# Attention block with routed experts: three issue orders changed (attention rows ahead of an expert's second weights, first half ahead of the differences in the search, two orders in the first selection)

## The reference, cut to what matters

```python
# x [2, 2048, 256]; 16 heads of 16; 8 experts of 128 slots, hidden 1024
h = _layernorm(x) * (1 + ca) + sa
q, k, v = heads(h @ Wq + bq), heads(h @ Wk + bk), heads(h @ Wv + bv)
scores = einsum('bhqd,bhkd->bhqk', q, k) * scale
sparsity = scores.max(-1) - scores.mean(-1)
_, top_idx = top_k(sparsity, 307)                 # per batch and head
attn = softmax(q[top_idx] @ k.T * scale)
out = zeros_like(q).at[top_idx].set(attn @ v)
x = x + ga * (merge(out) @ Wo + bo)

h = _layernorm(x) * (1 + cb) + sb
xn, sn = rmsnorm(h), rmsnorm(slot_embeds)
logits = einsum('bnd,esd->bnes', xn, sn)
dispatch, combine = softmax(logits, over n), softmax(logits, over e*s)
slots = einsum('bnd,bnes->besd', xn, dispatch)
eo = gelu(slots @ w1[e] + b1[e]) @ w2[e] + b2[e]
x = x + gb * einsum('bmd,bnm->bnd', eo, combine)
```

## Time and profile before

| | |
|---|---|
| runs, median | 1568.8 us (1565.49 to 1570.86) |
| profiled execution | 1565.02 us |
| its span | 1563.3 us |
| PE busy | 1456.9 us (93%) |
| DVE busy | 1214.3 us (78%) |
| ACT busy | 1042.3 us (67%) |
| POOL busy | 242.9 us (16%) |
| chain that ended last | PE 49%, DVE 34%, issue 11%, DMA 3%, ACT 2%, POOL 1% |

### The profile page before, as it was taken

The page is one execution under the profiler, slowest core; times in us unless marked ns, Lnnn a source line. Parts: engine busy times, 40 slices in busy tenths (PEclk is TensorE's granted clock), DMA queues, the critical chain, the costliest instruction groups (busy, mean ns, idle before and its releaser), DMA issues.

```text
span 1563.3 us, 28260 instructions
## 1 busy us (share of the span) xinstructions
PE 1456.9 (93%) x8706; PEld 802.8 (51%) x8706; DVE 1214.3 (78%) x2841; ACT 1042.3 (67%) x1452; POOL 242.9 (16%) x289
## 2 busy tenths in 40 slices
PE   7999999998989989999999889999999999999999
PEld 3542222223444432222222644444889986489988
DVE  5679999999897769999999888977855534775411
ACT  4578888887767778888888448864433463443453
POOL 1540000000720051111111212232111000011100
PEclk9999999999999999999999899999999999999999
DMA  5861111112432201111112212201243202024410
GB/s 178 267 170 41 41 40 41 41 43 84 148 119 79 69 18 50 48 42 42 42 42 82 71 40 60 54 24 46 94 162 126 95 30 74 1 85 153 136 49 32
DMA packets 93811, 119.40 MB, mean 76 GB/s; under 512 B 23054, under 2 KB 79118, under 8 KB 93212
## 3 DMA queue, kind: packets, MB, share of 16 engines
q1 hardware_dynamic: 91164, 117.66, 24.8%
q0 software_dynamic: 2560, 0.66, 0.2%
HBM read 93.46 MB, written 24.82 MB: 76 GB/s over the span
## 4 chain that ended last, share of the span: by engine, by line
PE 49%; DVE 34%; issue 11%; DMA 3%; ACT 2%; POOL 1%; SPq 0%; DVEq 0%; ACTq 0%
DVE work_area L1326 26%; PE psum L2181 7%; PE psum L2122 7%; PE psum L2245 7%; PE psum L2040 5%; PE psum L2031 4%; PE psum L2192 4%; PE psum L2012 3%; DVE big_area L1326 3%; PE psum L2201 2%; DMA work_area<-heads_out 2%; PE psum L2235 2%; PE psum L1833 1%; PE psum L1858 1%; DVE work_area L1398 1%
## 5 line engine op out<-in xcount | busy, mean ns | idle before, releaser
L1326 DVE CUSTOM_DVE_ANT_0 work_area<-psum,work_area 128x1024 f32<-128x1024 f32 x512 | 589.0, 1220 | 7.6 <-PE psum L1894 4.0
L910 ACT ACTIVATE work_area<-psum 128x1024 f32<-128x1024 f32 x512 | 510.1, 1027 | 74.5 <-DVE big_area L1326 30.3
L1894 PE MATMUL psum<-work_area 96*128 96x512 bf16 x1024 | 309.2, 384 | 47.9 <-DVE big_area L1326 6.8
L1884 PE MATMUL psum<-work_area 96*128 96x512 bf16 x1024 | 305.4, 380 | 7.4 <-ACT work_area L910 1.7
L1894 PEld LDWEIGHTS psum<-work_area 96*128 96x128 bf16 x1024 | 63.4, 97 | 266.3 <-DVE big_area L1326 243.8
L1884 PEld LDWEIGHTS psum<-work_area 96*128 96x128 bf16 x1024 | 88.7, 98 | 153.0 <-ACT work_area L910 58.6
L932 ACT ACTIVATE work_area<-psum 128x614 f32<-128x614 f32 x160 | 102.2, 682 | 29.3 <-PE psum L2031 27.1
L2181 PE MATMUL psum<-work_area,xn 128*128 128x128 f32 x1024 | 117.4, 275 | 0.5 <-ACT work_area L1022 0.5
L2181 PEld LDWEIGHTS psum<-work_area,xn 128*128 128x128 f32 x1024 | 115.8, 192 | 0.8 <-ACT work_area L1022 0.7
L2245 PE MATMUL psum<-expert_out,work_area 128*128 128x256 f32 x512 | 115.5, 379 | 0.0
L2122 PE MATMUL psum<-slots_T,work_area 128*128 128x512 f32 x256 | 115.0, 592 | 0.0
(11 more groups left out here) (271 smaller groups left out, 2049.4 us busy)
## 6 DMA issues: line engine op xcount, KB each, us to landing
work_area<-in_L_ffn_w_dram SPq DMA_DIRECT2D x32, 1024.0 KB, 5.2
work_area<-k_parts SPq DMA_DIRECT2D x192, 64.2 KB
work_area<-q_parts SPq DMA_DIRECT2D x192, 64.0 KB
k_parts<-work_area SPq DMA_DIRECT2D x24, 384.0 KB, 3.4
q_parts<-work_area SPq DMA_DIRECT2D x16, 384.0 KB, 2.9
big_area<-q_parts SPq DMA_DIRECT2D x16, 384.0 KB, 5.2
work_area<-k_parts SPq DMA_DIRECT2D x32, 192.0 KB
x_res<-in_L_attn_x_dram SPq DMA_DIRECT2D x8, 512.0 KB, 6.2
```

The source lines that it names most:

```text
L910: s.activation(SC[:, t % 4], PS[:, 2 * (n % 2):2 * (n % 2) + 2].rearrange("p a n -> p (a n)"), ACT.Relu).then_inc(relu_done, 1)
L1326: v.tensor_tensor_reduce(SC[:, t % 4], PS[:, 4 + 2 * (t % 2):6 + 2 * (t % 2)].rearrange("p a n -> p (a n)"), SC[:, t % 4], 1.0, -3.0e38, A ...
L1884: last = mm(PS[:, 2 * (n % 2) + k], QS1[par][0:TERMS, t * P:(t + 1) * P], KS[par][0:TERMS, k * 512:(k + 1) * 512], start=True, stop=True)
L1894: last = mm(PS[:, 4 + 2 * (t % 2) + k], QS1[par][0:TERMS, t * P:(t + 1) * P], KS[par][0:TERMS, K1 + k * 512:K1 + (k + 1) * 512], start=Tru ...
```

## The change

Three places of the code are written in another order; no arithmetic is changed. SP issues the rows for expert e+1 directly behind W1 of expert e, for e from 1 on. In the search PE issues the first half of tile t ahead of the differences of tile t+2. In the first selection POOL's four normalising instructions for token group 3 stand one each behind the third parts of units 3 to 6, where all four stood behind unit 3; and ACT takes a token group behind the natural queries of the next round and ahead of its `first_part`, where it stood directly behind the `first_part` of the unit that opened it.

```diff
@@ weights(b) on SP
                     sp.dma_start(W1, w1[e].rearrange("(c p) n -> p c n", p=P)).then_inc(w1_in, 16)
+                    if b == 0 and e:
+                        for t in expert_tiles(e + 1):
+                            head_rows(1, t)
                     sp.wait_ge(eo_ready, b * E + e)
                     sp.dma_start(W2, w2[e].rearrange("(j p) n -> p j n", p=P)).then_inc(w2_in, 16)
-                    if b == 0:
-                        for t in expert_tiles(e + 1) if e else range(4, HOLE + 4):
+                    if b == 0 and e == 0:
+                        for t in range(4, HOLE + 4):
                             head_rows(1, t)
@@ normalised(b, k) on POOL
-            def normalised(b, k):
+            def normalised(b, k, tiles=range(G)):
-                for j in range(G):
+                for j in tiles:
-                last.then_inc(xhat_ready, 1)
+                if G - 1 in tiles:
+                    last.then_inc(xhat_ready, 1)
@@ POOL's program
                 third_part(1, u)
-                if u == 3:
-                    normalised(1, 3)
+                if 3 <= u < 3 + G:
+                    normalised(1, 3, (u - 3,))
@@ first_part(b, u) on ACT
-                if turns(b, u):
+                if b == 0 and turns(b, u):
                     take_tokens(b, g + 1)
@@ ACT's program, rounds of the first selection
                 take_natural(0, q)
+                if turns(1, q):
+                    take_tokens(1, UNITS[q][0] + 1)
                 for u in share(q):
                     first_part(1, u)
@@ pe_maxima(i, par, last) on PE
                     for t in range(NT):
+                        first_half(i, par, t)
                         if t + AHEAD <= NT:
                             differences(i, par, t + AHEAD)
                         elif not last:
                             differences(i, par + 1, t + AHEAD - NT - 1)
-                        first_half(i, par, t)
```

## The result

The changed kernel takes 1557.5 us (median of 6 runs, 1557.0 to 1558.4) against 1568.7 us (6 runs, 1565.5 to 1570.9) for the kernel before: a ratio of 0.9933, with a 95% interval of 0.992 to 0.9946. Its profiled execution took 1558.07 us (span 1556.3, mean clock 0.992), only 7.0 us less than the 1565.02 us of the execution profiled before (mean clock 0.993). So two questions stand: where the 7.0 come from, and why the medians lie 4 us further apart.

The account below looks back on a forecast made before the run. No engine bounds the whole: row transfers bound the experts, DVE the search and the selection's rounds. 4.4 + 2.3 + 0 + 2.4 = 9.1 us off 1568.8 gives 1559.7 us, 8 in 10 between 1554.5 and 1566.

Parts of the forecast that it names:

- Rows ahead of the second weights, 4.4: Experts of batch 0: PE's turns no longer wait for rows, five loops get 4.4 us shorter.
- A: Search: the waits between heads go too, up to 5.7 us more won, 1554 us; chance 0.12.
- B: Experts: PE waits for ACT's gelu or tokens' sums instead of rows, 4.4 falls to about 0, 1564.1 us; chance 0.10.
- E: Experts: SP is held by `aoT_ready` ahead of W2, with the forecast's time even then; chance within the forecast's 0.64.
- Start of the search, 2.3: Both searches: DVE's first maximum comes 1.17 and 1.16 us earlier, together 2.3 us.
- rival D: First selection: a stretch at the lower PE clock appears, up to 5 us more, 1564.8 us; chance 0.07.
- Changes of heads, 0: Search, 30 head changes: the 0.19 us delay stays, nothing gained; bounds -5.7 and +3.0 us.
- First selection, 2.4: First selection: DVE's 1.60 us wait for POOL goes and ACT's copy comes earlier, 2.4 us; bounds 1.0 and 3.4.
- The sum: Whole kernel: 9.1 us less, a median of 1559.7 us, -0.58%.
- Rival C: Search: later relus lengthen every tile, slower than before, 1580 us at 0.04 us a tile; chance 0.05.

Follow-up runs that it names:

- the mirror image: The kernel before with the new search order for all tiles but the very first of each search: 1569.9 us, ratio 1.0016.
- The half tile computed twice: The kernel before plus an early, unsignalled copy of each search's first half tile, overwritten at the old place: 1566.14 us, ratio 0.9996.
- the versions with one and with two tiles: The kernel before with only the first tile, or first two tiles, of each search computed first half first: 1568.41 and 1568.53 us.

## Why the prediction was right, and where it was off

**Rows ahead of the second weights, 4.4:** right. 4.43 in the trace, both with the whole change and with the rows alone, and 4.15 by the medians of the latter. Rivals A, B and E did not come: no other wait stands in the chain in place of the one removed, and SP was not held up.

**Start of the search, 2.3:** right in the trace (1.05 and 1.14 by the distance from relu to maximum, 2.2 in span with the order alone), and too small for the time: the order alone gave 4.4 by the medians. The step that was off is the one that took the gain from one execution: the profiled execution of the kernel before had no stretch at the half clock at the second search, and other executions of the same program have one. Three of the six traces in which nothing fills PE's first wait of the search show it there: the second one of the kernel before (above), the rows alone and the mirror image, here in this order:

```profile
566.00:570.00 4.00, 4.00 (x10) 1.46 (x11) 1.46 (x3) 2.87 (x3) 4.00 (x1) 0.50 0.00 0
```

```profile
570.00:574.00 4.00, 4.00 (x11) 1.26 (x10) 3.34 (x7) 2.04 (x2) 4.00 (x1) 0.51 0.00 0
```

None of the eight traces does in which a half tile is computed there, the one computed twice among them. The runs point the same way: a mean clock of 0.990 or less is found in 38 of 71 runs of the kernel before, in 18 of 31 with the rows, the split pieces or the tokens alone, and in 1 of 61 with that half tile. The half tile computed twice separates the clock from DVE's start, which it leaves where it was: the low clocks went. That its time went down with them is not shown, as its interval includes no change and its transfers waited longer.

How the 4.4 come about is seen in two traces near their medians, the second one of the kernel before (1567.56) and that of the order alone (1562.85), whose spans are 4.7 us apart. The first search starts 1.14 us sooner behind its relu, and from the second search's first relu to its last maximum it is 296.15 us for 299.69, 3.5 less: 1.2 from the start and 2.3 from the clock. The other stages come out even. Against the first trace of the kernel before it is 1.2 alone. So 2.2 us are what the earlier starts give, and 2.3 more is what an execution with the stretch loses.

That this is the whole of the medians' 4.4 is not shown. Whether a run had the stretch is not on record, only its mean clock, and on the chip of the order alone 13 of 27 runs of the kernel before were at 0.990, just short of the half that would move a median by the whole 2.3. At one mean clock, 0.992, three runs of the order alone took 1562.63 to 1562.85 us and eight of the kernel before 1565.76 to 1566.78: some 3.8 apart, where the earlier starts give 2.2. What makes the other 1.6 is open; that the new order within the heads has a part in it is a rival that the mirror image, with its longer transfers and its late start, does not rule out. The stretch that went is rival D's mechanism with the other sign. The prediction had it in one sentence, by the Trainium skill ("TensorE: Matmul & The Clock Gate", section HAM oscillation), that taking PE's waits away "could as well spare a stretch", and put no number or chance on it. The traces agree with that rule, in that the stretch follows PE's waits at the turn from the attention to the search, and show beside it that the same program has it in some executions and not in others.

**Changes of heads, 0:** right, 0.20 us a head as before, so neither bound was touched. But the order within the heads is no ornament: the old order gives the lead back tile by tile, as the versions with one and with two tiles show. The prediction treated the start as if it stood by itself.

**First selection, 2.4:** mis-sized, 1.4 measured. That DVE "wants it a round and a half on" was right for the first part, and that "the unit that needs the tokens is four rounds off" was right for PE's unit; but DVE's own mean of the hidden rows reads the last tokens too, and earlier, and was not looked for. It waits 0.81 us for them. Without the late tokens the same 0.9 us is lost in another way, beside a piece of POOL. With the mean a unit later 2.2 of the 2.4 are there. So the replay that gave 2.4 left out one reader.

**The sum:** 9.1 forecast against 7.0 between the profiled executions and 11.1 between the medians. The forecast of 1559.7 lay 2.2 above the time, within its range, and that is luck in part: an overestimate of 1.0 in the selection was outweighed by some 2 us at the searches that no term held (2.3 of clock, if the median run of the kernel before had the stretch; the clocks of its six runs here are not on record). The 0.9 left is within what the medians of six runs can tell, as the ratio's interval is 2 us to either side. Rival C (a slower search) had nothing behind it.

## What to carry to other kernels

Before a change is priced against a profiled execution, compare its time and its mean clock with those of the other runs: this one was 2 to 4 us below the median, and a stretch at the half clock that another execution had, at a cost of 2.3 us, was not in it. Where TensorE waits at the start of a stage and another engine is the bound afterwards, work that is due anyway is well put into that wait: here it gave its own time back, and the executions at the lower mean clock went with it. When a value is delivered later, list every reader of it on every engine, small ones too, and when a start is advanced, follow the lead tile by tile until it is either kept or lost.

## What the runs showed of the hardware that was not expected

- A DVE instruction of two f32 numbers per partition takes 0.17 us alone and 1.08, 1.09, 0.57 and 0.44 us when it starts within a running POOL instruction of 1.15 us, in four versions; it ends when that one does. The reduction just ahead of it (0.15 to 0.16 us, in two of the four within POOL's piece) and the maxima are not slowed. The Trainium skill ("GPSIMD Engine Reference", section Key points) says that POOL shares its SBUF interfaces with DVE, with contention in a 2-port mode or with two SBUF inputs; the rows agree that there is contention, here for an instruction with one SBUF input; whether it ran in such a mode no trace tells.
- The granted clock falls to half at the same places of the program in every trace (near 445, 861 and 916 us) and at others only in some executions: near 55, 416, 565 and 1374 us, in one to three traces each.
- The order of PE's program ahead of the loop, with no change in any transfer, went with waits for DMA that were 1.5 to 3 us longer 600 us later. The cause is open.
